# Postnorm decoder layer on one core: the norms' products moved to VectorE, later weights' roundings to ScalarE, and the side stages placed anew

## The chip, the cores and the metric

One core of a Trainium2 chip runs the whole layer in one launch. The metric is the device time of that launch in microseconds (us), lower is better. The engines are PE (TensorE, matrix products and transposes), DVE (VectorE), ACT (ScalarE), POOL (GpSimd) and SP (SyncE, which only issues DMAs). Each engine works through its own instruction queue in the order in which the program was written; they meet only at semaphores.

## What is computed

For x of shape (4, 512, 512), with a layer norm (mean and variance over the last axis, no weights) behind each of three parts:

```python
x = layernorm(x + attention(x, Wq, Wk, Wv, Wo))          # 32 heads of 64, 8 kv heads, rope, causal softmax
x = layernorm(x + experts(x, fside, ctx))                # one int8 "smooth quant" expert per batch
x = layernorm(x + ffn(x, sign(up), sign(down), scales))  # 512 -> 2048 -> 512, relu
```
```python
def smooth_quant_linear(x, w):
    s = sqrt(max(amax|x| over rows, EPS) / max(amax|w| over rows, EPS)), at least EPS
    xs, ws = x / s, w * s
    x_scale, w_scale = max(amax of each row of |xs|, |ws|, EPS) / 127
    x_q, w_q = clip(round(xs / x_scale)), clip(round(ws / w_scale))
    return x_q @ w_q.T * x_scale * w_scale.T
# expert: h = smooth_quant_linear(x, fside); a = silu(gate) * up; smooth_quant_linear(a, ctx)
```

## The kernel before

Products that need more than one pass are made of a high part and a low part (`_hi`, `_lo`): ACT copies the high part, DVE or POOL subtracts it from the full value to get the low part, and PE multiplies the pairs.

**Attention** goes through 16 steps `g`: eight key/value heads for batches 0 and 1 (`half` 0), then the same eight for batches 2 and 3 (`half` 1). A step has two batches `b` and four query heads `h`, so 128 heads in all. In each head PE transposes the last head's probabilities (`ps_t`, L1752), makes the next head's scores (`ps_s`, L1707), a piece of the output projection into the bank `m1`, a projection into `m0`, and the products with the values (`ps_o`, L1764). DVE, in each head: `pT_lo` (L1433) three times, the row maxima of the next head's scores (`probs,neg_max`, L1372, `softmax_max`) four times, two of them before and two of them behind the second and third `pT_lo`; `add_o` (L1380); `add_y`, which adds a piece of the output projection to `y` (L1395); the inverse sums `r_inv` (L1455); and, by head, `normalize` (L1386) and the rotations of q. ACT takes the exponentials (L1162) and the high parts. POOL does the low parts of q, k, the weights and the output (`o_lo`, L980), the rotations of k, and `r_rep` (L964). Once a half of a pair of heads is done, PE spreads its inverse sums into the bank `m1` (`recips`, L1774); that product waits until `add_y` has read the bank.

**The side chains.** While half 1 of the attention runs, the 64 heads of it are "ticks" 0 to 63, and the layer norm and the expert of batches 0 and 1 are worked in between. The chain `N` of a batch is its first norm: `var0` to `var3` and `rstd` on DVE, `power` (the inverse root, L1091) on POOL, and `norm0` to `norm3`, the product `(y - mean) * rstd` of 128x512 each (`centered`, L1037) on POOL. `A` is the first linear of the expert: `wmax` of the transposed weights, `colmax` of `y`, `colx`, `ratio`, `root`, `reps`, `rowsw`, `rowsx`, the scaled `xs` (DVE) and `ws` (POOL), their row maxima `xabs`, `wabs`, the scales, the roundings `xround` and `wround` (add and scale, L1034 on POOL, L1255 on ACT), `xq`, `wq` (DVE), transposes `xT`, `wT` on PE, and four `prod`. `B` is the second linear with the same stages in half the width, then `add` (POOL), `var2`, `rstd2` (DVE), `power` and `y20` to `y23` (POOL, the second norm's product by the same `centered`), and `x2T0` to `x2T3` on PE with `hi` on ACT and `lo` (L1639) on DVE, which make the transposed input of the feed forward.

Tables of text give the tick and the place of each stage; `PLACED` puts them together, and each engine's function `later(place, tick)` emits what the table has there. For DVE the place `dve` lies in the middle of a head, between the first `pT_lo` and the second, and `dve2` behind the inverse sums:

```python
if k == 0 and half == 1:
    later("dve", slot(g, b, h))
```

**The feed forward** follows. For each of four batches it has 16 hidden tiles, so that two ticks (64 on) are one tile: eight `up` matmuls of 128x512 into `m0` (L1994), `hid` and `hid_hi` on ACT, `hid_lo` on POOL (L1030), and eight `down` matmuls into `ps_s` and `ps_t` (L2008) one tick later. `T` is the rest of the output projection of batch 3, `S` the signs of the weights, and `F` the last norm of a batch (`scale` DVE, `add` POOL L1105, `var` DVE, `power` POOL, `norm` DVE L1678, store). The chains of batches 2 and 3 (`A2`, `B1`, `A3`, `B2`, `B3`) run beside the tiles; the up matmuls of batch b wait for the last `lo` of `B` of that batch. `feed` emits the tiles, then `later` the stages of the tick.

Small operations on 128x4 or 128x2 (`scales` L1483, `ratio`, `reps` L1495, `inverse`, `variance`) are `tensor_scalar` with a constant, followed by a reciprocal or a product.

## Time and profile before

| | |
|---|---|
| median of 3 runs | 1498.04 us (1497.72 to 1505.10) |
| profiled execution | 1497.09 us |
| its span, first to last instruction | 1495.3 us |
| mean granted PE clock over the span | 0.964 of full speed |
| busy in the span | PE 1315.8 (88%), weight loads 1085.3, DVE 972.3 (65%), ACT 891.4 (60%), POOL 860.7 (58%) |
| heads 0 to 63 (half 0) | 0 to 560.5 us |
| heads 64 to 127 (half 1, ticks 0 to 63) | 560.5 to 1128.6 us |
| feed forward | 1128.6 to 1495.3 us |

A time beside a name is the start of an instruction from the span's start. An instruction's idle time is that of its engine just before it, with the one whose semaphore came last. Matmuls overlap: one of 128x512 is shown with 0.39 us, and the next starts 0.23 us after it. The profile's granted clock is 1.0 at 2.4 GHz and 0.5 at 1.2 GHz.

### The profile page before, as it was taken

How to read it: one execution, taken by the hardware profiler on the slowest of the kernel's cores; microseconds unless marked ns; L12 is line 12 of the kernel's file. 1: busy time of each engine (PE TensorE's matmuls, PEld its weight loads, DVE VectorE, ACT ScalarE, POOL GpSimd, SP SyncE). 2: the span in 40 equal slices, each digit the busy share in tenths (PEclk: the TensorE clock that was granted, in tenths of full speed). 3: DMA queues.
4: the chain of work that ended last, by engine and by line, in shares of the span. 5: the costliest groups of instructions: out<-in, count | busy, mean ns of one | idle time of the engine just before them, and what ended most of it. 6: DMA issues, size and time to landing. Idle time of an engine off the chain costs nothing.

```text
span 1495.3 us, 25046 instructions
## 1 busy us (share of the span) xinstructions
PE 1315.8 (88%) x7112; PEld 1085.3 (73%) x7112; DVE 972.3 (65%) x2391; ACT 891.4 (60%) x2120; POOL 860.7 (58%) x735
## 2 busy tenths in 40 slices
PE   3799999999999999899998999988879577988896
PEld 2688878888788877777787877776767455676675
DVE  3477777677777668788877878768765627634022
ACT  2576777767776766666776666655665453433332
POOL 3465565565664765756784555585514764747443
PEclk9899999999999999999999999999989798999998
DMA  4422222222222223212222223212234011100000
GB/s 177 149 77 50 59 57 72 75 54 56 56 67 63 77 86 106 57 50 61 54 76 63 68 80 88 61 48 52 54 137 184 1 43 43 43 14 29 0 29 28
DMA packets 54853, 98.78 MB, mean 66 GB/s; under 512 B 11744, under 2 KB 13792, under 8 KB 53728
## 3 DMA queue, kind: packets, MB, share of 16 engines
q1 hardware_dynamic: 54752, 97.57, 22.8%
q8 instruction: 47, 0.77, 0.2%
q14 instruction: 54, 0.44, 0.1%
HBM read 51.39 MB, written 4.19 MB: 37 GB/s over the span
## 4 chain that ended last, share of the span: by engine, by line
PE 56%; DVE 13%; POOL 13%; issue 9%; ACT 7%; DMA 0%; DVEq 0%; ACTq 0%; POOLq 0%; SPq 0%
PE m L1707 21%; PE ps_o L1764 7%; PE ps_s L1707 7%; PE m L1994 5%; PE ps_t L1752 5%; POOL y L1037 3%; PE ps_s L2008 3%; DVE probs L1372 3%; PE ps_t L2008 3%; DVE pT_lo L1433 2%; ACT pT_hi L1170 2%; PE m L1774 2%; POOL y L1105 1%; POOL o_lo L980 1%; ACT probs L1162 1%
## 5 line engine op out<-in xcount | busy, mean ns | idle before, releaser
L1162 ACT ACTIVATE probs<-probs,neg_max 128x128 f32<-128x128 f32 (+3 forms) x512 | 285.2, 559 | 192.6 <-DVE neg_max L1372 192.4
L1433 DVE TENSOR_TENSOR pT_lo<-ps_t,pT_hi 128x512 fp32r<-128x512 f32 (+1 forms) x384 | 220.1, 595 | 180.4 <-ACT pT_hi L1170 178.3
L1372 DVE CUSTOM_DVE_ANT_0 probs<-ps_s,mask 128x128 f32<-128x128 f32 (+3 forms) x512 | 228.3, 482 | 6.5 <-PE ps_s L1707 6.2
L1752 PE MATMUL ps_t<-ident,probs 128*128 128x128 f32 x1280 | 187.6, 278 | 50.3 <-DVE pT_lo L1433 29.3
L1707 PE MATMUL ps_s<-k_st,q_st 128*128 128x256 f32 (+2 forms) x1024 | 231.0, 348 | 0.3 <-DVE neg_max L1372 0.3
L980 POOL TENSOR_TENSOR o_lo<-o_sum,o_hi 128x512 fp32r<-128x512 f32 x64 | 81.9, 1280 | 223.0 <-ACT o_hi L1184 222.8
L1752 PEld LDWEIGHTS ps_t<-ident,probs 128*128 128x128 f32 x1280 | 148.4, 142 | 75.7 <-DVE pT_lo L1433 39.3
L1170 ACT ACTIVATE pT_hi<-ps_t 128x512 fp32r<-128x512 f32 (+1 forms) x384 | 186.1, 519 | 8.6 <-PE ps_t L1752 5.3
L1764 PE MATMUL ps_o<-pT_hi,v_st 128*128 128x256 f32 (+2 forms) x512 | 171.9, 346 | 2.1 <-DVE pT_lo L1433 2.1
L1030 POOL TENSOR_TENSOR hid_lo<-hid,hid_hi 128x512 fp32r<-128x512 f32 x64 | 82.2, 1287 | 136.6 <-ACT hid_hi L1337 136.6
L1764 PE MATMUL ps_o<-pT_lo,v_st 128*128 128x256 f32 (+2 forms) x512 | 157.6, 329 | 0.0
L1707 PEld LDWEIGHTS ps_s<-k_st,q_st 128*128 128x128 f32 x1024 | 151.6, 191 | 3.0 <-DVE neg_max L1372 0.5
L1335 ACT ACTIVATE hid<-m,up_col 128x512 f32<-128x512 f32 x64 | 43.9, 686 | 149.7 <-PE m L1994 149.7
L1177 ACT ACTIVATE o_part<-ps_o 64x512 f32<-64x512 f32 x128 | 75.8, 592 | 78.5 <-PE ps_o L1764 76.1
L1707 PE MATMUL m<-xT_hi,wqT_hi 128*128 128x512 f32 x256 | 102.2, 399 | 16.7 <-DVE xT_lo L1400 15.1
L1707 PE MATMUL m<-woT_hi,o_hi 128*128 128x512 f32 x256 | 106.0, 414 | 10.0 <-POOL o_lo L980 5.4
L1764 PEld LDWEIGHTS ps_o<-pT_hi,v_st 128*128 128x128 f32 x512 | 99.0, 193 | 13.0 <-DVE pT_lo L1433 3.4
L1764 PEld LDWEIGHTS ps_o<-pT_lo,v_st 128*128 128x128 f32 x512 | 99.2, 194 | 7.5
L1707 PE MATMUL m<-xT_hi,wqT_lo 128*128 128x512 f32 x256 | 101.9, 398 | 0.0
L1707 PE MATMUL m<-xT_lo,wqT_hi 128*128 128x512 f32 x256 | 101.8, 398 | 0.0
L1707 PE MATMUL m<-woT_lo,o_hi 128*128 128x512 f32 x256 | 101.6, 397 | 0.0
L1707 PE MATMUL m<-woT_hi,o_lo 128*128 128x512 f32 x256 | 101.5, 397 | 0.0
(246 smaller groups left out, 3111.3 us busy)
## 6 DMA issues: line engine op xcount, KB each, us to landing
q_st<-q_tmp SPq DMA_DIRECT2D x512, 64.0 KB, 2.0
raw<-in_wq_t SPq DMA_DIRECT2D x32, 256.0 KB, 3.0
k_st<-k_st SPq DMA_DIRECT2D x64, 128.0 KB, 2.3
raw<-in_wo_t SPq DMA_DIRECT2D x32, 256.0 KB, 2.9
raw_b<-in_ffn_t SPq DMA_DIRECT2D x10, 512.0 KB, 7.1
y<-in_x_t SPq DMA_DIRECT2D x4, 1024.0 KB, 9.5
raw<-in_wkv_t SPq DMA_DIRECT2D x16, 256.0 KB, 3.5
y<-in_x SPq DMA_DIRECT2D x4, 1024.0 KB, 6.1
```

The costliest lines, as they stand in the source:

```text
L980: pool.tensor_tensor(o_lo[:, buf, p, :], o_sum[:, :], f32(o_hi[:, buf, p, :]), ALU.subtract).then_inc(o_los, 1)
L1030: pool.tensor_tensor(hid_lo[:, n % 2, :], hid[:, n % 2, :], f32(hid_hi[:, n % 2, :]), ALU.subtract).then_inc(hid_los, 1)
L1162: act.activation(probs[:, h % 2, SO[i]:SO[i] + SW[i]], probs[:, h % 2, SO[i]:SO[i] + SW[i]], ACT.Exp, bias=neg_max[:, h % 2, i:i + 1], sca ...
L1170: act.activation(pT_hi[:, PT_FIRST[k]:PT_FIRST[k] + w, :], ps_t[:, (h + k) % 2, 0:P * w].rearrange("p (w c) -> p w c", c=P), ACT.Copy).the ...
L1177: act.activation(o_part[a:a + HD, :], ps_o[c:c + HD, :], ACT.Copy).then_inc(o_copied, 1)
L1372: dve.tensor_tensor_reduce(out=probs[:, h % 2, SO[i]:SO[i] + SW[i]], in0=ps_s[:, i % 2, 0:SW[i]], in1=mask[:, L - SW[i]:L], scale=-SCALE, ...
L1433: dve.tensor_tensor(pT_lo[:, d, :], ps_t[:, (h + k) % 2, 0:P * w].rearrange("p (w c) -> p w c", c=P), f32(pT_hi[:, d, :]), ALU.subtract).t ...
L1707: i = pe.matmul(dst, a, c, start=(j == 0), stop=(j == len(terms) - 1))
L1752: i = pe.transpose(ps_t[:, (h + k) % 2, P * c:P * (c + 1)], probs[:, h % 2, at:at + P], ident[:, :])
L1764: i = pe.matmul(ps_o[:, q0:L], v_st[:, buf, kt, v0:v0 + P], pT[:, blocks, :], start=(j == 0 and s == 0), stop=(j == 3 and s == 1))
L1994: i = pe.matmul(m0[:, :], w[:, P * k:P * (k + 1)], x2[:, b % 2, k, :], start=(k == 0 and x2 is xT_hi), stop=(k == KT - 1 and x2 is xT_lo))
L2008: i = pe.matmul(down_bank(t), hd[:, m % 2, P * t:P * (t + 1)], w[:, D:2 * D], start=(h == 0 and hd is hid_hi), stop=(h == HT - 1 and hd is ...
```

## The change

1. `centered` is emitted on DVE, not on POOL: the products `norm0` to `norm3` of all four `N` chains and `y20` to `y23` of all four `B` chains, 32 of 128x512. POOL keeps `power`. `x2T` of a tile waits for that tile's `y2` alone, where it waited for `y23`.
2. `wround` of batches 2 and 3 of `A` (8 of 128x512) and of batches 1 to 3 of `B` (12 of 128x256) goes from POOL to ACT.
3. The place `dve` in the middle of a head is gone. `dve1` is behind the inverse sums, `dve2` at the end of the head. On PE `pe1` is new, at a head's start; `pe2` and `pe3` are the old `pe` and `pe2`. POOL's places are as they were, but for that of the third head, which follows that of the second.
4. Small operations with a constant read it from a tile `bounds` and are `tensor_tensor`; `scales` has one more of them.
5. Stages are cut finer: `xs`, `xabs` and `wabs` of `A` by 512 columns, `xq`, `wq` and `a` in two, all of `B`'s `colmax`, `xs`, `xabs`, `wabs` in two, and `scale`, `add`, `var`, `norm` of `F` in four.
6. `inv_a` has two buffers, so that `wmax` of `A1` runs before `A0`'s weights are reloaded (`A1.wT` at tick 7, `A0.w` at 11). Waits for the shared bank `pc` are worked out from the table (`PC_USES`, `pc_free`).
7. The two tables `ATTENTION` and `FEED_FORWARD` take the place of all the old ones; nearly every stage has another tick.

```diff
-            def centered(n, mv, inv, t):
-                return pool.tensor_scalar(y[:, n, :], y[:, n, :], mv[:, t, 0:1], inv[:, 1, t:t + 1], ALU.subtract, ALU.mult)
...
+            def centered(n, mv, inv, t):
+                return dve.tensor_scalar(y[:, n, :], y[:, n, :], mv[:, t, 0:1], inv[:, 1, t:t + 1], ALU.subtract, ALU.mult)
...
                             if k == 0 and (prev or h > 0):
                                 add_o(n - 1, (h - 1) % G, u * 2 + (h - 1) // 2)
-                            if k == 0 and half == 1:
-                                later("dve", slot(g, b, h))
...
                         dve.reciprocal(r_inv[:, :, h // 2, h % 2], row_sum[:, h % 2, :]).then_inc(r_done, 1)
                         if half == 1:
-                            later("dve2", slot(g, b, h))
+                            later("dve1", slot(g, b, h))
...
                             if b == 0 and prev:
                                 add_y(g, b, half, "out3 early")
+                        if half == 1:
+                            later("dve2", slot(g, b, h))
...
+                elif name[:6] == "wround":
+                    after(act, "A", "dve", b, "wscale")
+                    i = scale_round(w_gu, sm_a, 7, [int(name[6])], D)
...
             def scales(sm, j):
-                link(dve.tensor_scalar(sm[:, j, :], sm[:, j, :], EPS, 1.0 / QMAX, ALU.max, ALU.mult))
+                link(dve.tensor_tensor(sm[:, j, :], sm[:, j, :], bound(0, QT), ALU.max))
+                link(dve.tensor_tensor(sm[:, j, :], sm[:, j, :], bound(1, QT), ALU.mult))
                 return dve.reciprocal(sm[:, j + 1, :], sm[:, j, :])
...
             def reps(sm, kt):
-                link(dve.tensor_scalar(sm[:, 3, 0:kt], sm[:, 3, 0:kt], EPS, None, ALU.max))
+                link(dve.tensor_tensor(sm[:, 3, 0:kt], sm[:, 3, 0:kt], bound(0, kt), ALU.max))
...
                     t = int(name[3])
-                    if t == 0:
-                        after(pe, "B", "pool", b, "y23")
+                    after(pe, "B", "dve", b, f"y2{t}")
...
-    47 pool power y20
-    48 pool y21 y22
-    50 pool y23
+    50 dve1 B0.y20
+    50 dve2 B0.y21
+    50 pool1 B0.power
+    51 dve1 B0.y22
+    51 dve2 B0.y23
```

Three places of the order show it. DVE, attention, the head in which the stage `reps` of `A1` stands before (tick 48): `L1380` is `add_o`, `L1495` and `L1496` are the stage, `L1433` the second and third `pT_lo`, `L1372` the last maxima, `L1395` `add_y`, `L1455` the inverse sums. Before:

```order
L1380 TENSOR_TENSOR o_sum<-ps_o,o_part 64x512
L1495 TENSOR_SCALAR sm_a<-sm_a 128x4
L1496 RECIPROCAL sm_a<-sm_a 128x4
L1433 TENSOR_TENSOR pT_lo<-ps_t,pT_hi 128x512
L1433 TENSOR_TENSOR pT_lo<-ps_t,pT_hi 128x256
L1372 ISA probs,neg_max<-ps_s,mask 128x384
L1372 ISA neg_max 128x1
L1372 ISA probs,neg_max<-ps_s,mask 128x512
L1372 ISA neg_max 128x1
L1395 TENSOR_TENSOR y<-y,m 128x512
L1455 RECIPROCAL r_inv<-row_sum 128x4
L1386 TENSOR_TENSOR o_sum<-o_sum,m 128x512
```

The same head in the change (its lines are `L1538`, `L1476`, `L1499`, `L1558`, `L1490`; the stages there now are `xs` of `A1`, `L1658`):

```order
L1538 TENSOR_TENSOR pT_lo<-ps_t,pT_hi 128x256
L1476 ISA probs,neg_max<-ps_s,mask 128x384
L1476 ISA neg_max 128x1
L1476 ISA probs,neg_max<-ps_s,mask 128x512
L1476 ISA neg_max 128x1
L1499 TENSOR_TENSOR y<-y,m 128x512
L1558 RECIPROCAL r_inv<-row_sum 128x4
L1658 TENSOR_TENSOR xs<-y,pc 128x512
L1490 TENSOR_TENSOR o_sum<-o_sum,m 128x512
L1459 TENSOR_TENSOR q_tmp<-m,sin_sb 128x512
L1460 TENSOR_TENSOR q_tmp<-m,cos_sb 128x512
L1658 TENSOR_TENSOR xs<-y,pc 128x512
```

The stage stood ahead of the maxima and of `add_y`; now one stands behind the inverse sums and one behind all of the head's own work.

POOL, feed forward, first batch: `L1049` scales the weights of `A2`, `L1074` and `L1075` those of `B1`, `L1091` and `L1037` are `power` and the products of `N3`, `L1030` is `hid_lo`, `L1034` `wround`. Before:

```order
L1049 TENSOR_TENSOR w_gu<-w_gu,cm 128x512
L1074 TENSOR_TENSOR w_dn<-w_dn,cm_b 128x256
L1075 TENSOR_TENSOR w_dn<-w_dn,cm_b 128x256
L1091 TENSOR_TENSOR norm_n<-norm_n,half_pow 128x4
L1037 TENSOR_SCALAR y<-y,mv_n,norm_n 128x512 x4
L1049 TENSOR_TENSOR w_gu<-w_gu,cm 128x512
L1030 TENSOR_TENSOR hid_lo<-hid,hid_hi 128x512
L1034 TENSOR_SCALAR w_gu<-w_gu,sm_a 128x512 x2
L1034 TENSOR_SCALAR w_dn<-w_dn,sm_b 128x256 x4
```

In the change (`L1152`, `L1177` and `L1178`, `L1136` in the same roles):

```order
L1164 TENSOR_TENSOR sm_b<-sm_b,half_pow 128x2
L1152 TENSOR_TENSOR w_gu<-w_gu,cm 128x512 x2
L1136 TENSOR_TENSOR hid_lo<-hid,hid_hi 128x512
L1177 TENSOR_TENSOR w_dn<-w_dn,cm_b 128x256
L1178 TENSOR_TENSOR w_dn<-w_dn,cm_b 128x256
L1177 TENSOR_TENSOR w_dn<-w_dn,cm_b 128x256
L1178 TENSOR_TENSOR w_dn<-w_dn,cm_b 128x256
L1136 TENSOR_TENSOR hid_lo<-hid,hid_hi 128x512
L1152 TENSOR_TENSOR w_gu<-w_gu,cm 128x512
```

The products of the norm and the roundings are no longer between the scalings and `hid_lo`.

PE, feed forward, end of the first batch, in the change: `L2043` are products of `A2`, `L1984` all four `x2T` of `B1`, `L2105` the first up matmuls of the next batch. Before, each `x2T` (`L1861`, four transposes) had eight matmuls of a tile between it and the next.

```order
L2043 MATMUL m<-wqT,xqT 128x512 x4
L2043 MATMUL ps_o<-wqT,xqT 128x512 x4
L1984 MATMUL pc<-ident,y 128x128 x16
L2105 MATMUL m<-xT_hi,sgn_a 128x512
L2105 MATMUL m<-xT_lo,sgn_a 128x512
```

The four now stand behind each other, with no tile between.

## Rows read from the trace of the kernel before

**Rows 1.** Windows (steady step, half 1): length, PE, PEld, DVE, ACT, POOL busy (instructions), clock, DMA
```profile
240.60:304.00 63.40, 61.10 (x355) 52.24 (x353) 45.97 (x127) 45.10 (x117) 36.55 (x31) 1.00 0.24 62
560.50:1128.60 568.10, 509.93 (x2903) 427.05 (x2901) 433.28 (x1105) 373.63 (x945) 335.47 (x285) 0.97 0.26 72
```
**Rows 2.** Waits of the steady step: us in total, times, longest
```profile
DVE pT_lo L1433 <- ACT pT_hi L1170: 10.3, 9, 2.1
ACT probs L1162 <- DVE neg_max L1372: 9.5, 11, 1.3
```
**Rows 3.** Waits of half 1 of the attention
```profile
ACT probs L1162 <- DVE neg_max L1372: 116.5, 98, 7.5
DVE pT_lo L1433 <- ACT pT_hi L1170: 92.6, 62, 4.1
PE m L1774 <- DVE y L1395: 23.8, 16, 5.7
```
**Rows 4.** Timeline, head at tick 48: start, us, engine, line, [idle before]
```profile
982.96 4.12 POOL L1037 TENSOR_SCALAR y<-y,mv,norm 128x512 f32<-128x512 f32 x2
988.12 1.23 DVE L1495 TENSOR_SCALAR sm_a<-sm_a 128x4 f32<-128x4 f32 x1 [4.73 <-POOL sm_a L1042]
991.12 0.61 ACT L1162 ACTIVATE probs<-probs,neg_max 128x384 f32<-128x384 f32 x1 [7.51 <-DVE neg_max L1372]
992.35 1.12 PE L1774 MATMUL m<-ident,r_rep 128*128 128x128 f32 x4 [5.65 <-DVE y L1395]
```
**Rows 5.** Timeline, head at tick 53: a small stage of A1 and POOL's work beside it
```profile
1033.62 4.01 DVE L1483 TENSOR_SCALAR sm_a<-sm_a 128x4 f32<-128x4 f32 x1
1035.09 2.51 POOL L952 TENSOR_TENSOR q_tmp<-q_tmp 128x512 fp32r<-128x512 f32 x2
```
**Rows 6.** Windows of the feed forward: the four batches of tiles
```profile
1128.60:1253.00 124.40, 92.14 (x426) 69.03 (x427) 65.32 (x105) 55.02 (x76) 70.26 (x55) 0.86 0.18 68
1253.00:1340.30 87.30, 78.00 (x374) 58.54 (x372) 49.70 (x78) 36.82 (x56) 56.64 (x49) 0.95 0.07 25
1340.30:1421.10 80.80, 70.00 (x306) 54.01 (x305) 25.59 (x44) 28.16 (x45) 45.83 (x38) 0.94 0.04 14
1421.10:1478.50 57.40, 55.75 (x241) 44.94 (x240) 10.16 (x17) 19.77 (x31) 25.19 (x20) 1.00 0.05 19
```
**Rows 7.** Timeline of the feed forward: POOL, DVE and PE
```profile
1179.27 8.25 POOL L1037 TENSOR_SCALAR y<-y,mv_n,norm_n 128x512 f32<-128x512 f32 x4
1188.77 1.22 DVE L1487 TENSOR_REDUCE sm_a<-w_gu 128x2 f32<-128x1024 f32 x1 [9.23 <-POOL w_gu L1049]
1191.58 1.03 PE L1868 MATMUL ps_o<-ident,xq 128*128 128x128 bf16 x8 [13.85 <-DVE xq L1557]
1232.48 1.11 PE L1861 MATMUL pc<-ident,y 128*128 128x128 f32 x4 [8.73 <-POOL y L1037]
1235.95 0.63 PE L2008 MATMUL ps_t<-sgn_b,hid_hi 128*128 128x512 f32 x1
1249.17 0.80 PE L1994 MATMUL m<-xT_hi,sgn_a 128*128 128x512 f32 x1 [5.16 <-DVE xT_lo L1639]
1313.14 0.80 PE L2008 MATMUL ps_s<-sgn_b,hid_hi 128*128 128x512 f32 x1 [3.48 <-POOL hid_lo L1030]
```
**Rows 8.** Waits of the feed forward
```profile
PE ps_s L2008 <- POOL hid_lo L1030: 15.9, 6, 6.1
PE pc L1868 <- DVE xq_b L1614: 3.8, 2, 3.5
```
**Rows 9.** Instructions by line: ns min/median/max, first and last start
```profile
L1037 POOL TENSOR_SCALAR y<-y,mv_n,norm_n x16: 2066/2074/3130, 613.6 to 1185.4; 128x512 f32<-128x512 f32 x16
L1678 DVE TENSOR_SCALAR y<-y,mv_f,norm_f x16: 533/546/1585, 1283.4 to 1491.6; 128x512 f32<-128x512 f32 x16
L1255 ACT ACTIVATE xs<-xs,round_col,sm_a x8: 798/802/816, 1173.2 to 1272.8; 128x512 f32<-128x512 f32 x8
L1492 DVE TENSOR_TENSOR sm_a<-sm_a,inv_a x4: 161/162/166, 652.5 to 1255.8; 128x4 f32<-128x4 f32 x4
L1573 DVE TENSOR_TENSOR av_f<-xs x3: 1207/1216/1706, 1160.0 to 1307.9; 128x1024 f32<-128x1024 f32 x3
```

1061 lines of the change are left out of this document (582 added, 479 removed).

## The prediction

> **What bounds the kernel now.** I read the windows first, then the waits, then the timeline around the longest of them. PE is the engine that sets the end wherever the others keep up. A steady step of half 0 takes 63.40 us and PE is busy for 61.10 of them [rows 1], so there is nothing to win in half 0, which the change hardly touches. Half 1 takes 568.10 us where eight steady steps would take 8 x 63.4 = 507.2: an excess of 60.9. PE's own busy time is 509.93 against 8 x 61.10 = 488.8, so 21.1 of the excess is work of the side chains (and some slow clock), and 39.8 is PE standing still more than it does in half 0.
>
> The feed forward takes 1495.3 - 1128.6 = 366.7 us. PE is idle for 124.4 - 92.1 = 32.3, then 9.3, 10.8 and 1.7 us in the four batches of tiles [rows 6]: 54 us. Its mean granted clock there is 0.86, 0.95, 0.94 and 1.00, so some of the busy time is at the lower level of 1.2 GHz. The last 16.8 us, behind 1478.5, are the last norm and its store. Together PE waits for about 94 us that other engines could in principle cover, and the question is how much of it this change removes.
>
> *Attention.* The waits of half 1 [rows 3] hold one that belongs to the place of the stages: the spread of the inverse sums waits for `add_y` 16 times, 23.8 us in all. The head at tick 48 shows how [rows 4]. POOL works on `y2` products, so `root` is late; the stage `reps`, in the middle of DVE's head, waits 4.73 us for it and takes 1.23; the third and fourth maxima and `add_y` stand behind it; ACT waits 7.51 for a maximum and PE 5.65 for `add_y`. ACT's wait for maxima is 116.5 us in half 1, against 9.5 x 8 = 76 at the steady rate [rows 2, 3]: 40 more, which agrees with PE's 39.8.
>
> *Feed forward.* The two largest stops are in the first batch [rows 7]. POOL does the four products of `N3` in 8.25 us between two scalings of `A2`'s weights; DVE waits 9.23 for the scaling, and PE 13.85 for an `xq` that stands behind it. 41 us later PE waits 8.73 for the four `y2` of `B1`. After each, PE's matmuls run at 1.2 GHz for a while: the one at 1235.95 takes 0.63 us instead of 0.39.
>
> **The change, part by part.** The sum is made against the profiled execution, 1497.09 us; the median of the three runs is 0.95 above it.
>
> *The place in the head.* With `dve1` behind the inverse sums and `dve2` behind the whole head, no stage of a head stands before that head's maxima or `add_y`. I take the whole 23.8 us of PE's wait for `add_y` as gone. What the moved stages now delay is `normalize`, the rotation of q, and the next head's first `pT_lo`. DVE is idle before `pT_lo` for 10.3 us in a steady step, 1.3 a head [rows 2], and for 92.6 in half 1, because the late exponentials only move that idle time [rows 3]. That is the cover. The table puts up to three `xs` at one head's end, and some ten heads are over 1.3 us by about 0.4, so I give back 4 us. Without the cover all the stages' time would come back: DVE is busy for 433.28 us in half 1, 8 x 45.97 = 367.8 of it the attention's own, so 65.5 us of stages [rows 1].
>
> *The products on DVE.* In attention 12 of them leave POOL at 2.07 us each, 24.8 us. On DVE the same operation is there already in the last norm: median 0.55, at worst 1.59 [rows 9]. 12 cost 6.6 to 19 us of DVE, beside the same idle time. I take the lower end for the clock and nothing for the path, since they stand at heads' ends; the upper end goes into the range. `reps` no longer waits behind `y2` at tick 48, which is a part of the 23.8 and is not counted again. Attention: 23.8 - 4 = 20 us less.
>
> *First batch of tiles.* POOL loses the 8.25 us of `N3` between the scalings, and `A2`'s transposes stand nine ticks later, so the 13.85 goes. The 8.73 becomes the first `y2` alone, 0.55 to 1.59 us. After both stops eight matmuls ran 0.43 us apart instead of 0.23, 1.6 us each time. That is 13.85 + 8.73 - 1 + 3.2 = 24.8. Against it stand the four `x2T` in one place: each needs PE, then ACT, then DVE before the bank is free, and DVE has other stages between the four `lo`. By the order PE would be idle there for about 7 us and slow after it, where it was idle 1.3 + 5.16 before [rows 7]. With 2 us more there and some of the gain lost to stages that are late for another reason, I take 20.
>
> *Other batches.* PE waits 15.9 us for `hid_lo` in six places [rows 8]. The two longest, 6.1 and the one at 1313.14 with 3.48 [rows 7], are behind `y2` products, and go: 9.6. The rest is mostly behind the four `add` of the last norm, which now stand apart: half of it, 2.6. `xq_b` is 3.8, nearly all in one wait behind `ws`, and clock after the 6.1 another 1.8. That makes 17.8; I take 16. The end of 16.8 us stays. Feed forward: 36 us less.
>
> *The roundings on ACT.* 8 of 128x512 at 0.80 us [rows 9], and 12 of half the width that cost no more: below 16 us on an engine that is busy for 120 of 292 us in the first three batches of tiles [rows 6]. `hid` needs about 1.3 us per tile, and the roundings are one to four in a tick. Nothing on the path, if `wscale` is done when ACT comes to them; if it isn't, `hid` waits, the more so because the whole tile waits for it.
>
> *Small operations.* The one at 1033.62 took 4.01 us while POOL ran operation after operation [rows 5]; an undisturbed `tensor_tensor` of that size takes 0.16 [rows 9]. On the path I count nothing beyond the 23.8 in which it is. **The Trainium skill**, page "SBUF — State Buffer", section "Who interferes with whom", says that DVE shares a port pair with GpSimd, that a two-port mode takes it, and that an instruction with two SBUF inputs contends as well with a GpSimd instruction that reads SBUF, the loser being fully blocked. By that rule the new small `tensor_tensor`, with two SBUF inputs, would wait as the old ones did, and the product at 0.55 us would wait whenever POOL works. Rows 9 hold both: no slower small `tensor_tensor` than 0.166 us, but one of 128x1024 at 1.71 instead of 1.21.
>
> Sum: 1497.09 - 20 - 36 = 1441; with the median's 0.95 I predict **1442 us**.
>
> **Rivals.**
> - *Only POOL's stops go.* The stages at heads' ends cost as much as those in the middle: each is still DVE time between one head's exponentials and the next head's `pT_lo`. For it: DVE's 433 of 568 us leave little, and the table puts more stages into the first 32 heads than before. Against it: in the old place even a short stage holds ACT and PE [rows 4]. Attention then gains 5, the feed forward 20, since the four `x2T` in one place and `hid` behind the roundings take the rest: 1497 - 25 = 1472.
> - *PE comes near its floor.* Stages placed apart on all engines leave no long stop: 36 of the 39.8 in attention and 50 of the 54 in the feed forward go, 1497 - 86 = 1411. For it: hardly any stop is a true dependence, most are queue order. Against it: the chain from `A1` to `x2T` of `B1` must still fit into one batch of tiles.
> - *The products starve on DVE, slower.* 32 products that POOL never had to wait with are now of the kind that took up to 1.59 us beside POOL [rows 9], and a small one took 4.01 beside back-to-back POOL work [rows 5]. If a product takes 2.9 us instead of 0.55 and stands on the path, 32 x 2.35 = 75 us come back, and 1441 becomes 1516. It decides from 0.55 + 56/32 = 2.3 us per product on. Against it: POOL has 66 us less to do, and 15.9 of the waits of PE were behind POOL. The skill's rule of full blocking speaks for this case, and its time is the one given here.
> - *The stages in effect stay where they were* (a place moved, waits turned into others of equal length): 1490 to 1505, slightly either way.
>
> **How the numbers follow.** The forecast, 1425 to 1460, has 0.60. PE near its floor has 0.14, only POOL's stops 0.14, no net change 0.05, starved products 0.07. The predicted time is that of the first. The range must leave out no more than 2 in 10: from 1415, which cuts off about half of the floor's case, to 1480, which takes in the second end of POOL's case and leaves out the last two. A measurement of this kernel can tell about 0.5%, 7.5 us, from no change. Faster by more than that: 0.60 + 0.14 + 0.14 and a little of the rest, 0.89; within it 0.04; slower 0.07.
>
> **What would show it.** In the changed kernel's profile the spread of the inverse sums (the product from `r_rep`) should wait for `add_y` for under 5 us in all, half 1 should take about 548 us and the first batch of tiles about 104, with the others at 80, 72 and 57. No POOL group for the products, 48 products by the line of `centered` on DVE with a mean below 1.2 us. The four `x2T` of `B1` should show PE idle for 6 to 8 us. Small operations should be at 0.2 us with no 4 us among them. I am wrong if half 1 takes over 560 us, or if the mean product is above 2.3 us, or if ACT's `hid` shows waits behind its own roundings with PE idle for it.

## The result, and the profile after

The changed kernel takes **1410.45 us** (median of 4 runs, 1408.63 to 1410.71), beside 1501.57 us (1497.72 to 1506.46) for the kernel before on the same chip: a ratio of 0.9389, 95% interval 0.9353 to 0.9425. The forecast was 1442 with a range of 1415 to 1480, so the sign was right, the size was not, and the time lies below the range. It is the time that the rival "PE comes near its floor" gave (1411, chance 0.14). The profiled execution took 1410.46 us, span 1408.6, mean granted clock 0.981 for 0.964 before. Stretches and waits below are each of one execution, and executions of one kernel differ by up to 12 us (1463.93 to 1475.62 in e5; the profiled one of before, 1497.09, is at the low end of its own), so by stretches the gain is 86.7 us and by the ratio 92.

The windows of the changed kernel: half 1, the four batches of tiles and the end, in the columns of [rows 1, 6].

```profile
563.60:1100.70 537.10, 500.23 (x2890) 423.17 (x2894) 447.93 (x1141) 374.83 (x945) 310.42 (x273) 0.98 0.28 74
1100.70:1197.40 96.70, 87.97 (x430) 66.01 (x434) 79.20 (x138) 59.84 (x84) 40.76 (x35) 0.96 0.28 99
1197.40:1270.90 73.50, 72.95 (x371) 57.37 (x373) 55.99 (x99) 41.46 (x63) 43.66 (x37) 0.99 0.09 29
1270.90:1336.30 65.40, 64.97 (x305) 51.50 (x305) 31.28 (x54) 29.93 (x48) 35.98 (x30) 1.00 0.05 17
1336.30:1391.80 55.50, 55.50 (x242) 45.09 (x241) 10.01 (x17) 19.81 (x30) 25.45 (x20) 1.00 0.05 19
1391.80:1408.60 16.80, 3.92 (x16) 2.56 (x15) 7.86 (x17) 1.32 (x2) 7.23 (x6) 0.76 0.17 62
```

Half 1 is 31.0 us shorter (568.1 to 537.1), the feed forward 58.8 (366.7 to 307.9): batch by batch 27.7, 13.8, 15.4 and 1.9, the end of 16.8 unchanged. Half 0 is 3.1 longer (560.5 to 563.6), but that isn't the change's: kernels below with the same half 0 took 561.8 to 564.7. Two things fell at once. PE's idle time went from 58.2 to 36.9 us in half 1 and from 54.0 to 9.7 in the four batches. And its busy time fell, for the same matmuls: 509.93 to 500.23 in half 1, and by 14.5 in the batches.

The waits of half 1, then those of PE in the feed forward (total, times, longest), which answer to [rows 3, 8]:

```profile
ACT probs L1257 <- DVE neg_max L1476: 75.2, 85, 3.4
DVE pT_lo L1538 <- ACT pT_hi L1265: 55.9, 53, 3.0
PE ps_t L1873 <- DVE pT_lo L1538: 20.3, 18, 3.7
PE m L1895 <- DVE y L1499: 4.2, 2, 2.4
...
PE pc L1984 <- DVE xT_lo L1759: 4.9, 3, 1.9
PE m L2105 <- DVE xT_lo L1759: 1.8, 2, 1.4
PE ps_s L2119 <- POOL hid_lo L1136: 1.0, 1, 1.0
```

The wait of the spread of the inverse sums for `add_y` has gone from 23.8 to 4.2 us, and ACT's for the maxima is down to the steady rate of 76. PE's 15.9 us behind `hid_lo` are down to 1.0, and the 13.85 behind `xq` and the 8.73 behind `y2` are gone. What is left in the feed forward is the turn of the four `x2T`. What is new is PE's wait for `pT_lo`, 20.3 us with stops up to 3.7; before it was 14.9. Three heads, at ticks 5, 21 and 37, take 12.35, 12.0 and 12.5 us where a head of their kind takes 6.65.

### The profile page after: what moved, and what is told of

Read it like the earlier page. It is cut to its first block, busy times and chain, and to the rows that moved or that the text cites. A ratio compares the mean times of both kernels' runs of the same rounds, so it can differ in the third digit from the quotient of the medians.

```text
span 1408.6 us, 25177 instructions
## 1 busy us (share of the span) xinstructions
PE 1293.1 (92%) x7101; PEld 1075.5 (76%) x7112; DVE 1012.7 (72%) x2491; ACT 904.2 (64%) x2140; POOL 783.6 (56%) x686
## 4 chain that ended last, share of the span: by engine, by line
PE 75%; DVE 9%; ACT 6%; issue 5%; POOL 3%; DMA 1%; ACTq 0%; DVEq 0%; SPq 0%; POOLq 0%
PE m L1828 30%; PE ps_s L1828 9%; PE ps_o L1885 8%; PE m L2105 7%; PE ps_t L1873 7%; PE ps_s L2119 4%; PE ps_t L2119 3%; DVE pT_lo L1538 2%; PE m L1895 2%; ACT pT_hi L1265 2%; ACT probs L1257 1%; DVE o_sum L1490 1%; PE pc L1984 1%; DVE probs L1476 1%; POOL o_lo L1087 1%
## 5 line engine op out<-in xcount | busy, mean ns | idle before, releaser
L1538 DVE TENSOR_TENSOR pT_lo<-ps_t,pT_hi 128x512 fp32r<-128x512 f32 (+1 forms) x384 | 220.7, 595 | 143.4 <-ACT pT_hi L1265 141.2
L1476 DVE CUSTOM_DVE_ANT_0 probs<-ps_s,mask 128x128 f32<-128x128 f32 (+3 forms) x512 | 228.2, 482 | 6.6 <-PE ps_s L1828 6.6
L1885 PE MATMUL ps_o<-pT_hi,v_st 128*128 128x256 f32 (+2 forms) x512 | 168.7, 340 | 0.2 <-DVE o_sum L1484 0.2
L1136 POOL TENSOR_TENSOR hid_lo<-hid,hid_hi 128x512 fp32r<-128x512 f32 x64 | 83.0, 1297 | 133.7 <-ACT hid_hi L1441 133.6
L1828 PE MATMUL m<-xT_hi,wqT_hi 128*128 128x512 f32 x256 | 102.6, 401 | 18.3 <-DVE xT_lo L1504 16.7
## 6 DMA issues: line engine op xcount, KB each, us to landing
raw_b<-in_ffn_t SPq DMA_DIRECT2D x10, 512.0 KB, 6.8
```

Of the source, the lines that this page charges most:

```text
L1136: pool.tensor_tensor(hid_lo[:, n % 2, :], hid[:, n % 2, :], f32(hid_hi[:, n % 2, :]), ALU.subtract).then_inc(hid_los, 1)
L1476: dve.tensor_tensor_reduce(out=probs[:, h % 2, SO[i]:SO[i] + SW[i]], in0=ps_s[:, i % 2, 0:SW[i]], in1=mask[:, L - SW[i]:L], scale=-SCALE, ...
L1538: dve.tensor_tensor(pT_lo[:, d, :], ps_t[:, (h + k) % 2, 0:P * w].rearrange("p (w c) -> p w c", c=P), f32(pT_hi[:, d, :]), ALU.subtract).t ...
L1828: i = pe.matmul(dst, a, c, start=(j == 0), stop=(j == len(terms) - 1))
L1885: i = pe.matmul(ps_o[:, q0:L], v_st[:, buf, kt, v0:v0 + P], pT[:, blocks, :], start=(j == 0 and s == 0), stop=(j == 3 and s == 1))
```

## The experiments

Ratios are to the kernel before, run beside it. The stretches are of the profiled execution, in us; a batch is one of tiles. By "the table" is meant what the change did to the order of the stages beside the parts with a name: their ticks, the finer cuts and the waits worked out from them.

| kernel | ratio (95%) | half 0 | half 1 | batch 0 | batch 1 | batch 2 |
|---|---|---|---|---|---|---|
| before | 1 | 560.5 | 568.1 | 124.4 | 87.3 | 80.8 |
| changed | 0.9389 (0.9353 to 0.9425) | 563.6 | 537.1 | 96.7 | 73.5 | 65.4 |
| e1, norms on POOL | 0.9508 (0.9480 to 0.9536) | 562.6 | 542.2 | 103.8 | 77.8 | 72.2 |
| e2, roundings on POOL | 0.9420 (0.9395 to 0.9444) | 563.1 | 537.0 | 98.3 | 76.4 | 65.3 |
| e3, place in mid head | 0.9606 (0.9580 to 0.9631) | 564.7 | 571.3 | 96.8 | 73.4 | 65.4 |
| e4, unstarved | 0.9305 (0.9281 to 0.9329) | 564.1 | 527.0 | 96.9 | 73.2 | 65.4 |
| e5, before + place | 0.9784 (0.9739 to 0.9829) | 562.0 | 536.6 | 124.0 | 92.5 | 82.6 |
| e6, before + products | 0.9772 (0.9743 to 0.9801) | 563.5 | 561.3 | 110.7 | 87.1 | 72.1 |
| e7, before + three parts | 0.9646 (0.9616 to 0.9675) | 561.8 | 539.7 | 112.2 | 85.9 | 72.1 |
| e8, e1 and e2 together | 0.9554 (0.9520 to 0.9587) | 564.0 | 537.0 | 106.9 | 79.8 | 72.3 |
| e9, e4 + x2T between | 0.9298 (0.9279 to 0.9317) | 563.8 | 527.1 | 95.2 | 74.6 | 65.4 |
| e10, e4 + x2T later | 0.9278 (0.9256 to 0.9299) | 564.7 | 525.5 | 96.6 | 72.7 | 65.4 |
| e11, reduction at the place | 0.9344 (0.9321 to 0.9367) | 563.4 | 533.4 | 97.0 | 73.4 | 65.4 |
| e12, small constants | 0.9378 (0.9359 to 0.9397) | 563.7 | 539.8 | 96.1 | 72.2 | 65.4 |
| e13, eight stops in half 0 | 0.9551 (0.9527 to 0.9574) | 587.5 | 538.1 | 96.8 | 73.5 | 65.4 |
| e14, e7 + A2's xT later | 0.9635 (0.9609 to 0.9661) | 563.5 | 538.4 | 114.7 | 85.7 | 72.0 |
| e15, combined | 0.9298 (0.9275 to 0.9321) | 564.3 | 523.6 | 95.3 | 74.9 | 65.4 |
| e16, e14 + B1's xT later | 0.9662 (0.9631 to 0.9694) | 562.3 | 538.4 | 117.4 | 82.9 | 72.1 |
| e17, combined, one more | 0.9274 (0.9250 to 0.9299) | 563.3 | 523.4 | 95.5 | 74.1 | 65.4 |

### The place in the head

e3 puts VectorE's first place back, e5 gives it to the kernel before.

```diff
                             if k == 0 and (prev or h > 0):
                                 add_o(n - 1, (h - 1) % G, u * 2 + (h - 1) // 2)
+                            if k == 0 and half == 1 and slot(g, b, h) > 0:
+                                later("dve1", slot(g, b, h))
...
-                        if half == 1:
+                        if half == 1 and slot(g, b, h) == 0:
                             later("dve1", slot(g, b, h))
```

> The changed kernel with VectorE's first place of a head moved back to where it was before the change, behind the first lo part of the probabilities and ahead of the inverse sums (all heads but the first of the second half). Theory: the wait of the recips' transposes for add_y and of the probabilities for the maxima of the next head come back, as in the sum of the prediction: +15 to +25 us, all of it between 564 and 1101 us, none in the feed-forward. Rival B (the table, not the place): within 5 us of 1410. Rival D (the place costs in both directions, what is late is then the stages themselves): over +30.

> The kernel before with one part of the change alone: VectorE's first place of a head behind the inverse sums and the second at the head's end; tables, products, roundings and small operations stay as before. In the changed kernel the place was worth 34 us (the first place moved back gave half 1 of 571 us for 537). Theory (the place alone ends the waits behind add_y and the maxima, whatever the table): half 1 of 568 us goes to 540 to 548, so 20 to 28 us less than before, ratio 0.981 to 0.987. Rival G (place and table only work together, since stages that PE awaits in the same head are now late): within 5 us of before, or slower.

e3 lost 34.2 us in half 1 and e5 won 31.5, each with nothing else in half 1 changed, so **the place is worth all of the attention's 31.0 us**, and more than the prediction's theory or either expectation gave it. By its size e3 lands at its rival D, over 30 us, but 11.8 of the 34.2 are PE's busy time (512.0 for 500.2); its idle time rose by 22.4, which is within the 15 to 25 of the theory. PE's waits in e3's half 1, and the windows of half 1 in e5:

```profile
PE ps_t L1875 <- DVE pT_lo L1538: 21.5, 16, 4.3
PE m L1897 <- DVE y L1499: 18.3, 15, 3.5
```

```profile
562.00:1098.70 536.70, 500.25 (x2904) 422.42 (x2903) 426.32 (x1105) 374.46 (x945) 334.89 (x285) 0.98 0.27 75
```

The wait for `add_y` is there again with 18.3 us. In e5 PE's idle time falls from 58.2 to 36.5, by 21.7, close to what the prediction took (23.8 less 4); its busy time falls by 9.7 as well. But e5 lost 5.2 us in batch 1 and 1.8 in batch 2 without any change there. For batch 1 the traces show what goes with it, one small operation, the scale of `A3`; batch 2's stays open. Before, then e5, with POOL's last two operations beside it:

```profile
1268.48 0.72 DVE L1483 TENSOR_SCALAR sm_a<-sm_a 128x4 f32<-128x4 f32 x1
1238.13 3.88 DVE L1483 TENSOR_SCALAR sm_a<-sm_a 128x4 f32<-128x4 f32 x1
1239.45 2.52 POOL L1049 TENSOR_TENSOR w_gu<-w_gu,cm 128x512 f32<-128x512 f32 x2
```

It ends 0.03 us after POOL does. PE's two stops at the transposes of `xq_b` and `xq` behind it grow from 3.54 and 0.44 us to 4.08 and 2.10, and PE's busy time in the batch by 2.9. So that loss goes with an operation held beside POOL, as in the three long heads below. e7 and e14 have the same 3.88 us in a batch 1 of 85.9 and 85.7 us; e16 hasn't, in one of 82.9.

### The products, the roundings, the small operations

e1 moves the 32 products of the first norms and of the norms behind B back to POOL's queue, e2 the roundings of A2, A3 and B1 to B3, e8 both; e12 takes back the form of the small operations. Some lines of each table, and one of the operations:

```diff
 e1
-    94 pool1 B1.power
-    95 dve1 A3.wmax1 A2.prod1 B1.y20 B1.y21 B1.y22
+    94 pool1 B1.power B1.y20 B1.y21 B1.y22 B1.y23
+    95 dve1 A3.wmax1 A2.prod1
 e2
-    88 act1 B1.wrow A2.xround3 A2.wround0 A2.wround1
-    88 pool1 B1.add0
+    88 act1 B1.wrow A2.xround3
+    88 pool1 A2.wround0 A2.wround1 B1.add0
 e12
-                link(dve.tensor_tensor(sm[:, j, :], sm[:, j, :], bound(0, QT), ALU.max))
-                link(dve.tensor_tensor(sm[:, j, :], sm[:, j, :], bound(1, QT), ALU.mult))
+                link(dve.tensor_scalar(sm[:, j, :], sm[:, j, :], EPS, 1.0 / QMAX, ALU.max, ALU.mult))
```

> The changed kernel with one part undone: the 16 products of the first norms and the 16 of the norms behind the attention layers' second product go back to POOL, at the tick of their power; all other stages stay where the change put them. Theory (each of three parts removes stops of its own: products off POOL, the place in the head, the finer table): in the feed-forward half 24 products of 1.25 us stand before hid_lo again, so PE stops there; +10 to +20 us over the changed kernel's 1410, while two of the three long heads (12.3 us instead of 6.65) lose their cause, -11, and bursts of five POOL operations delay o_lo by some us each in two places. Sum: about 1420, between 1412 and 1430. Rival A (most of the gain is the products leaving POOL): 1455 or more. Rival B (the table alone gives the gain): 1400 to 1412.

> The changed kernel with the later layers' weight roundings (A2, A3, B1, B2, B3: 8 of 512 columns and 12 of 256) back on POOL at the same ticks, ahead of the additions there; nothing else. Theory: POOL gets about 8 x 1.25 + 12 x 0.65 = 18 us back in bursts of 1.3 to 2.5 us, each ahead of one hid_lo; about half shows as PE's wait: +8 us, 1418, with no change before 1100 us. Rival C (the roundings on ScalarE are a main part of the feed-forward's 59 us): +25 us or more. Rival B (the table alone): within 3 us of 1410.

> The changed kernel with the norms' products and the later layers' weight roundings both back on POOL. Alone they cost 19 and 3 to 5 us. Theory: they stand in the same queue ahead of hid_lo, in bursts of different ticks, so the sum: 22 to 26 us over the changed kernel, 1435 to 1440 (ratio to before 0.955). Rival J (POOL is near its limit in the feed-forward, so the second costs more than alone): 32 us or more.

> The changed kernel with the small operations as before: bounds and scales by constants in tensor_scalar (two bounds in one operation in the scales) instead of tensor_tensor with a tile of bounds. Theory (the form is worth nothing, as in the prediction's sum, since either form waits beside POOL): within 3 us of 1410 (ratio 0.937 to 0.941), with the long head at tick 37 as before. Rival M (the form by constants takes longer beside POOL, as the one of 4.01 us did): 6 us or more slower, small operations over 1.3 us in over six places.

e1 costs 18.1 us in the feed forward, as expected (there by 20 products of 2.07 us, not by the 24 of 1.25 of the expectation), and its half 1 took 5.1 more, where 11 less were expected: two of the long heads did go, but POOL's burst made another, of 17.6 us. The 5.1 themselves are not the products': e8 has the same program in half 1 and took 537.0 there. PE's waits in e1's feed forward, then POOL and VectorE in its head 3:

```profile
PE ps_s L2116 <- POOL hid_lo L1122: 12.5, 4, 4.7
PE pc L1981 <- DVE xT_lo L1756: 4.5, 3, 1.5
```

```profile
585.56 8.26 POOL L1129 TENSOR_SCALAR y<-y,mv_n,norm_n 128x512 f32<-128x512 f32 x4
593.78 1.26 POOL L1073 TENSOR_TENSOR o_lo<-o_sum,o_hi 128x512 fp32r<-128x512 f32 x1
595.15 0.68 DVE L1481 TENSOR_TENSOR o_sum<-ps_o,o_part 64x512 f32<-64x512 f32 x1 [6.54 <-POOL o_lo L1073]
```

Four products in one tick take 8.26 us, and whatever the path needs of POOL stands behind them: `hid_lo` there, as before the change [rows 8], and `o_lo` here, for which VectorE waits 6.54 us. e2 costs 4.5 us of feed forward. e8 costs 23.4 there, where the two alone make 22.6 (by the ratios 25 us in all, where they make 22.5), so they add up and rival J's 32 did not come. The small operations' form changes nothing that can be measured (e12): the one at the end of head 36 takes 3.27 us as a `tensor_scalar` and 3.26 as a `tensor_tensor`.

### The parts one by one from the other side

e6 gives the kernel before the products alone, e7 the products, the roundings and the place, with before's ticks and unsplit stages.

```diff
 N_FAST
-    2 pool power norm0 norm1 norm2 norm3
+    2 pool power
+    3 dve norm0 norm1 norm2 norm3
 B_FAST
-    8 pool wround0 wround1
+    8 act wround0 wround1
-    18 pool power y20 y21 y22 y23
+    18 pool power
+    19 dve y20 y21 y22 y23
```

> The kernel before with the norms' 32 products of y on VectorE, in the tick behind their power or the next ones, and nothing else. In the changed kernel they are worth 18 us of the feed-forward and 5 of the attention. Theory: the same here, feed-forward 366.7 to about 348, attention between -5 and +5 (products at VectorE's middle place delay the maxima by 0.55 us each): 18 to 25 us less than before, ratio 0.984 to 0.988. Rival A (with before's coarser table POOL's bursts of five cost more): 30 us or more. Rival H (products in the middle of a head starve as at ticks 4 and 20 of the changed kernel): attention 5 us or more longer for each.

> The kernel before with three parts of the change together: place, products on VectorE, later layers' roundings on ScalarE; before's table of ticks, stages unsplit, small operations by constants. What is left to the changed kernel is the table alone (finer stages, other ticks, waits for a bank's readers) and the small operations. Theory: place -25, products -20, roundings -4, sum 50 of the 92 us; the table is worth the other 40, nearly all in the feed-forward (ratio 0.966). Rival B' (the table gives under 10 us, and the three parts do together what they don't do alone): ratio 0.945 or less. Rival I (the table is nearly all): ratio 0.985 or more.

The products give 22.6 us of the feed forward (366.7 to 344.1) and 6.8 of half 1. Together that is 29 us, by the ratio of 0.9772 even 34, more than the 18 to 25 expected and about rival A's 30: with before's places the products cost more than in the changed kernel. Roundings add nothing in e7 (344.4 for 344.1), as far as two kernels can tell that each hold one small VectorE operation in batch 1, for 6.60 us in e6 and 3.88 in e7. With place, products and roundings the kernel has 53 of the 92 us; what is left is **the table: 36.5 us of the feed forward** (344.4 to 307.9), and 2.6 net in half 1, where it also made the three long heads. This was expected at 40, and e12 shows that the small operations have no share in it.

Which property of the table it is, e14 and e16 asked. In e7 PE stands 8.2 us at A2's `xT`, which it meets before VectorE has its `xq`. e14 places that stage five ticks later (with it `xq` three, `wq` and `wT` two and what follows one tick), e16 also B1's `xT` three ticks later (`wT` and `wrow` one).

```diff
-    10 pe xT0 xT1
-    11 act wround2 wround3 xqT0 xqT1
+    11 act wround2 wround3
+    15 pe xT0 xT1
+    15 act xqT0 xqT1
 B_FAST, for B1, in e16
-    8 pe xT
+    11 pe xT
```

> The kernel before with the three parts (ratio 0.9646, first batch of tiles 112.2 us), and in its table one chain delayed: A2's xT from tick 81 to 86, xq from 80 to 83, wT, wrow and the products behind it by one tick; nothing else. Theory (the table's gain is that PE meets no stage before its data are there; in before's table it meets A2's xT 8.2 us early): the 8.2 us stop is gone or under 2 us, half of it comes back as a denser end of the batch, first batch 104 to 108 us, ratio 0.959 to 0.962. Rival O (the chain itself is too long, and the wait moves to a later stage of it): within 2 us of 112.

> The kernel before with the three parts, A2's transposes later as in the run before (ratio 0.9635), and now B1's as well: its xT from tick 81 to 84, wT from 84 to 85, wrow from 85 to 86, products as before. Theory (PE meets both chains' stages before VectorE has got to them, so only both together help): 3 more ticks are about 7 us of tiles, the 9.15 us stop falls to 2 or less, first batch 114.7 to 106 to 109 us, ratio 0.957 to 0.960. Rival P (VectorE's queue from tick 72 to 92 is the bound of the batch, whatever PE's order; the wait moves to the products or x2T): first batch 112 to 116 us.

Both failed. In e14 the stop became one of 9.15 us at B1's `xT`; in e16 that one is gone too, and batch 0 is 117.4 us, longer than before either move. ScalarE's timeline in e16 shows what holds it now:

```profile
1150.36 2.08 ACT L1325 ACTIVATE av_f<-av_f,round_col,sm_b 128x256 f32<-128x256 f32 x4 [2.36 <-DVE sm_b L1561]
1152.34 1.04 ACT L1394 ACTIVATE sgn_b<-raw_b 128x1024 fp32r<-128x1024 f32 x1
1153.28 0.67 ACT L1412 ACTIVATE hid<-m,up_col 128x512 f32<-128x512 f32 x1
```

ScalarE meets the roundings before VectorE's scales are there, and `hid` stands behind them; it is the same again 6 us later, and PE waits 4.51 and 2.34 us for the two `hid`. That is what the prediction feared of the roundings; the changed kernel has no such wait of PE. So PE's early stage was one symptom of before's ticks, and two attempts to move single stages sent the stop to another engine's queue. That all the ticks are too early on every engine is a reading of these two runs and not shown. Whether the split of the stages or their ticks carries more of the 36.5 us stays open; it was not tried apart.

### The three long heads

The changed kernel at head 4's end: VectorE, POOL and PE from its timeline.

```profile
604.78 3.52 DVE L1618 TENSOR_SCALAR y<-y,mv_n,norm_n 128x512 f32<-128x512 f32 x1
608.23 0.68 DVE L1538 TENSOR_TENSOR pT_lo<-ps_t,pT_hi 128x512 fp32r<-128x512 f32 x1
...
604.31 1.27 POOL L1087 TENSOR_TENSOR o_lo<-o_sum,o_hi 128x512 fp32r<-128x512 f32 x1
605.55 1.25 POOL L1053 TENSOR_TENSOR q_tmp<-q_tmp 128x512 f32<-128x512 f32 x1
606.77 1.25 POOL L1054 TENSOR_TENSOR q_tmp<-q_tmp 128x512 f32<-128x512 f32 x1
...
608.96 0.69 PE L1873 MATMUL ps_t<-ident,probs 128*128 128x128 f32 x2 [3.59 <-DVE pT_lo L1538]
612.28 0.63 PE L1828 MATMUL m<-woT_lo,o_hi 128*128 128x512 f32 x1
```

The product starts 0.47 us after POOL's `o_lo` and ends 0.28 after the last of three POOL operations that follow each other without a gap. PE stands for 3.59 us, and then its matmul of 512 columns takes 0.63 instead of 0.39. At 741.15 the same happens again, and at 881.06 it happens to the scale of the down layer, a `tensor_tensor` of 128x4 (minimum, median, maximum of its line in ns):

```profile
L1618 DVE TENSOR_SCALAR y<-y,mv_n,norm_n x16: 516/541/3523, 592.8 to 1138.9; 128x512 f32<-128x512 f32 x16
L1591 DVE TENSOR_TENSOR sm_b<-sm_b,bounds x8: 151/340/3264, 881.1 to 1291.9; 128x4 f32<-128x4 f32 x8
```

e4 moves the three stages off that place, which lies behind the rotation of the queries; e11 leaves two and puts a reduction where the first stood.

```diff
 e4
-    4 dve2 N0.norm3
-    5 dve1 A0.wmax1
+    5 dve1 N0.norm3 A0.wmax1
-    20 dve2 N1.norm1
-    21 dve1 N1.norm2
+    21 dve1 N1.norm1 N1.norm2
-    36 dve2 B0.xscale
-    37 dve1 B0.wabs0
+    37 dve1 B0.xscale B0.wabs0
 e11
-    4 dve2 N0.norm3
-    5 dve1 A0.wmax1
+    4 dve2 A0.wmax1
+    5 dve1 N0.norm3
```

> The changed kernel with three stages moved by one place, from the end of a head to behind the inverse sums of the next: the fourth norm product of batch 0, the second of batch 1, and the scale of the down layer. Each of them began in the changed kernel while POOL ran two or three operations in a row behind the rotation of the queries and ended only after the last (3.52, 3.52 and 3.26 us instead of 0.54 and 0.16), and the head behind it took 12.0 to 12.5 us instead of 6.65. Theory (VectorE is starved there by POOL, and all of the long head comes from it): three heads of 6.65, -15 to -17 us, about 1394. Rival E (the op is long because what it reads or the queue is late, so the delay moves along): -5 us or less. Rival F (the ops are starved at the new place as well): no change.

> The changed kernel with two stages exchanged: at the end of head 4, behind the rotation of the queries, stands the maximum of weights A0.wmax1 (a reduction with one input from SBUF, 128x512 twice, about 1.2 us), and the fourth norm product stands where the maximum was, behind the inverse sums of head 5. Theory (what starves there is an operation with two inputs from SBUF or in the fast form, not any operation): the reduction runs its 1.2 us while POOL works, head 5 takes 6.7 to 7.6 us instead of 12.35, and the kernel 5 us less. Rival F' (whatever stands there is late while POOL runs three operations in a row): the reduction takes over 3 us and the head 12 or more.

e11, VectorE and POOL at the same place:

```profile
604.55 1.22 DVE L1626 TENSOR_REDUCE inv_a<-w_gu 128x2 f32<-128x1024 f32 x1
605.80 0.69 DVE L1538 TENSOR_TENSOR pT_lo<-ps_t,pT_hi 128x512 fp32r<-128x512 f32 x1
...
604.10 1.27 POOL L1087 TENSOR_TENSOR o_lo<-o_sum,o_hi 128x512 fp32r<-128x512 f32 x1
605.33 1.26 POOL L1053 TENSOR_TENSOR q_tmp<-q_tmp 128x512 f32<-128x512 f32 x1
```

The reduction starts in the middle of the same POOL work and isn't held: 1.22 us, and head 5 takes 7.31 us. Nor is, in the changed kernel, an `xs` with one input from PSUM at head 48's end:

```profile
984.42 0.69 DVE L1658 TENSOR_TENSOR xs<-y,pc 128x512 f32<-128x512 f32 x1
...
983.81 1.29 POOL L1087 TENSOR_TENSOR o_lo<-o_sum,o_hi 128x512 fp32r<-128x512 f32 x1 [0.24 <-ACT o_hi L1279]
985.05 1.31 POOL L1053 TENSOR_TENSOR q_tmp<-q_tmp 128x512 f32<-128x512 f32 x1
```

So it is the kind of operation that decides, at a place where POOL is busy. **The Trainium skill**, page "SBUF — State Buffer", section "Who interferes with whom", says that a `tensor_reduce` never contends on trn2, that an operation with two SBUF inputs and a `tensor_scalar` in a two-port mode can, and that the loser is fully blocked. Both timelines agree with it; which mode the products ran in no trace shows. Two inputs aren't needed: the same scale as a `tensor_scalar` with constants took 3.27 us (e12).

Nor is it the end of a head: the 4.01 us of [rows 5] stood in the middle of one, and e5's 3.88 and e6's 6.60 among the tiles. Over all the runs 25 such operations (small ones and products) took more than 3 us. Beside each of them POOL ran from one operation into the next, three to seven of them, and each ended 0.02 to 0.29 us after POOL's last. Nothing here shows why VectorE gets in between two POOL operations at other times.

In e4 all three heads are at 6.65 us or so, 17 us less, but half 1 fell by only 10.1: head 38, behind the scale that was moved, takes 10.39 us instead of 8.77, and the last 16 heads took 129.9 us where the changed kernel took 125.4. PE's stops there are of the same size in both (about 2.1, 1.8, 1.9 and 2.4 us). Windows of the same heads, 58 and 59, in the changed kernel and then in e4:

```profile
1054.50:1074.20 19.70, 13.93 (x93) 11.92 (x93) 13.88 (x36) 13.42 (x33) 4.02 (x4) 1.00 0.66 189
```

```profile
1040.40:1063.20 22.80, 17.05 (x92) 14.73 (x93) 13.99 (x36) 13.50 (x33) 3.96 (x4) 0.85 0.61 183
```

Idle time is the same, 5.8 us, and busy time 3.1 more at a clock of 0.85. It need not be another kernel for that. e1 and e8 have the same program in half 1; their windows of it:

```profile
562.60:1104.80 542.20, 502.07 (x2894) 424.59 (x2892) 434.85 (x1129) 375.09 (x945) 334.33 (x285) 0.98 0.28 74
564.00:1101.00 537.00, 496.84 (x2895) 419.66 (x2894) 434.95 (x1129) 375.19 (x946) 334.43 (x285) 0.99 0.28 74
```

PE is idle for 40.1 and 40.2 us, and busy for 5.2 more in e1, whose five executions lie at 1427 to 1428 us and at 1432 to 1433. The same stops cost the clock in one execution and not in another. So the 4.5 us of e4 can't be put down to what was moved, though its five executions agree within 1.8 us.

### What a stop costs

That led to e13: eight equal delays in half 0, where nothing else is in the way.

```diff
+                        if half == 0 and (b, h) == (1, 1):
+                            for j in range(6):
+                                dve.tensor_reduce(sm_b[:, j, 0:1], sin_sb[:, :], AX.X, ALU.max)
```

> The changed kernel with a known delay in half 0 alone: at the end of VectorE's seventh-last place, head 1 of the second fill in each of its eight steps, six added reductions of 128x512 from one SBUF tile (0.65 us each, 3.9 us, written to a tile that is overwritten later). VectorE is idle there for about 1.3 us, so PE should stand still for about 2.6 us eight times, 21 us. Theory (a stop costs more than itself, since the matmuls behind it run at 1.2 GHz for a while): half 0 takes 3.6 to 4.3 us more for each, 29 to 34 us in all, and PE's busy time in it rises by 5 to 12 us although its work is the same. Rival N (a stop costs its length or less): 21 us or less, PE's busy time the same within 2 us.

The six reductions took 3.64 us, and the stop was 1.91 us at seven of the eight places and 2.66 at the last; 2.6 was expected. Half 0 took 23.9 us more. The windows of e13 behind two of the stops, at 105.4 and at 171.4, and PE's timeline behind the second:

```profile
105.40:109.40 4.00, 4.00 (x18) 3.06 (x18) 3.94 (x13) 2.47 (x8) 0.00 (x0) 1.00 0.43 98
171.40:175.40 4.00, 3.99 (x14) 3.23 (x15) 3.94 (x13) 2.46 (x8) 0.00 (x0) 0.68 0.46 107
```

```profile
171.41 0.44 PE L1876 MATMUL ps_t<-ident,probs 128*128 128x128 f32 x2 [1.91 <-DVE pT_lo L1538]
172.54 0.40 PE L1831 MATMUL m<-xT_hi,wkvT_hi 128*128 128x512 f32 x1
173.59 0.63 PE L1831 MATMUL m<-xT_hi,wkvT_hi 128*128 128x512 f32 x1
```

Behind the first stop the clock stays at 1.00 and the head takes 10.60 us instead of 8.32: 2.3 more. Behind the second it falls to 0.68 over 4 us, a part of them at 1.2 GHz, and the head takes 11.98: 3.7 more. They alternate: four heads of the eight lost 2.3, three 3.7, the last 2.7. The windows from the head of the first stop to the end of half 0, in the changed kernel and in e13:

```profile
99.70:563.40 463.70, 445.80 (x2558) 380.00 (x2557) 333.52 (x914) 330.01 (x854) 273.38 (x233) 1.00 0.26 66
100.60:587.30 486.70, 452.70 (x2558) 382.39 (x2557) 361.29 (x962) 329.95 (x854) 273.63 (x233) 0.99 0.25 63
```

PE's idle time rose by 16.1 us (17.9 to 34.0) and its busy time by 6.9, for the same matmuls. **A stop of PE costs itself and, on average, two fifths more.** The theory had that right, in kind and in size: it asked for 5 to 12 us of busy time. The 29 to 34 us of half 0 did not come since the stops were shorter.

### Versions that beat both

e9 fills the turn of B1's four `x2T` with two products, e10 moves batch 0's `x2T` to PE's second place, e15 has both and the scale beside its `xabs1`, and e17 one stage more.

```diff
 e9
-    95 pe1 A2.prod2 A2.prod3 B1.x2T0 B1.x2T1 B1.x2T2 B1.x2T3
+    95 pe1 B1.x2T0 A2.prod2 B1.x2T1 A2.prod3 B1.x2T2 B1.x2T3
 e10
-    58 pe1 B0.x2T0
-    58 pe2 A1.wT0
-    58 act1 B0.hi0
-    58 dve1 B0.lo0
+    58 pe2 A1.wT0 B0.x2T0
+    58 act2 B0.hi0
+    58 dve2 B0.lo0
 e15
-    36 dve1 B0.xabs1
+    36 dve1 B0.xabs1 B0.xscale
 e17
-    97 pe1 B2.colx A3.colx
+    97 pe1 B2.colx
+    98 pe1 A3.colx
```

> The kernel with the three stages moved (1399 us here, ratio 0.9305), and in it the turn of batch 1's second norm: PE's last two products of A2 between the first three transposes x2T instead of ahead of all four, VectorE's four norm products ahead of them and its other stages behind the last lo, ScalarE's silu behind the four hi. Theory (each x2T stops PE for 1.4 to 1.85 us since it waits for ScalarE's hi and VectorE's lo of the one before, 6.3 us in all, and two stops can be filled with a product of 0.9 us each): 1.8 to 3.5 us less in batch 1's first tile (18.2 us) and up to 1 at 1.2 GHz, about 1396. Rival K (the chain is bound by VectorE's four norm products, which then stand ahead of it): no change or up to 2 us more.

> The kernel with the three stages moved (ratio 0.9305), and in it the four transposes x2T of batch 0 at PE's second place of heads 58 to 61 instead of the first, with their hi at ScalarE's and their lo at VectorE's end of the head. Theory (the first x2T waits 2.1 us at the head's start for the bank that v's lo part frees late, the fourth 1.1 for the lo before): 3 us less in heads 58 to 61 of 36.4 us. Rival L (the heads 58 to 62 lack work on PE, since the last step projects nothing for a next one, so a stop that is taken away comes back at the spread of the inverse sums, which waits 1.8 and 2.4 us for the sum of y): within 1 us of 1399.

> The changed kernel with all stages moved that the runs named: the three starved ones (the down layer's scale now beside its xabs1 in head 36, since at head 37 it made head 38 1.6 us longer), the four x2T of batch 0 at PE's second place, and the turn of batch 1's norm with two products between its x2T, B2's column maxima ahead of A3's. Theory: 1397.5 - 1.6 for head 38, - 1.7 for the first batch and no loss in the second: about 1394, between 1391 and 1397. Rival (ScalarE, the clock or other waits take it back, as heads 58 to 62 took 4.5 of 17 us): 1397 to 1400.

> The combined kernel (1397.6 us, ratio 0.9298) with the spread of A3's column maxima one tick later on PE, tick 98 instead of 97: it stood still there for 2.07 us. Theory: 1.5 to 2.1 us less in the second batch (74.9), about 1395.7, ratio 0.9285. Rival: within 0.5 us of the combined kernel, since the stop goes to the next stage.

e9 won 1.7 us in batch 0 and lost 1.4 in batch 1, so nothing. e10 won 1.5 us of half 1 where 3 were expected: two stops went, and the spread of the inverse sums waits 2.50 instead of 1.80, as its rival said. e15 came out at 1397.55, at the rival's time: half 1 was the best yet (523.6), but a new stop of 2.07 us stood in batch 1. e17 takes it away and has 1394.93 us (1394.68 to 1395.72), 0.9274 of before and 0.988 of the changed kernel by the two ratios. Its batch 1 is only 0.8 us shorter than e15's. Against e10, with a ratio of 0.9278, the lead is within the intervals. Its window of half 1:

```profile
563.30:1086.70 523.40, 495.73 (x2896) 419.07 (x2894) 439.62 (x1141) 374.36 (x945) 310.76 (x273) 0.99 0.28 76
```

## Why the prediction was wrong in size

*What bounds the kernel.* Right: half 0 had nothing to give, the stops of PE were where the gain lay, and the rows that were named as the largest (the wait for `add_y`, 13.85, 8.73, `hid_lo`) are those that went.

*Where it failed, first: the clock.* The step that failed is the term for PE's busy time. The sum took stops at their own length and added 3.2 us for the first batch ("eight matmuls ran 0.43 us apart instead of 0.23, 1.6 us each time") and 1.8 for the others; for the attention it added nothing. PE's busy time fell by 9.7 us in half 1 and 14.5 in the four batches, 24.2 against 5: **19 us of the error.** The mean granted clock in the batches rose from 0.86, 0.95 and 0.94 to 0.96, 0.99 and 1.00. Across kernels with the same matmuls in half 1, idle and busy time go together: 59.3 and 512.0 in e3, 58.2 and 509.9 before, 36.9 and 500.2 changed, 29.9 and 497.1 in e4, 27.7 and 495.7 in e17. 31.6 us less idle time went with 16.3 less busy time. e13 shows it caused, at two fifths; e1 and e8 show that 5 us of busy time come and go at the same idle time, so the share for one kernel is no closer than that. In the prediction the step "PE's own busy time is 509.93 against 488.8, so 21.1 of the excess is work of the side chains (and some slow clock)" should have set the work apart from the clock.

*Second: the stops that were to stay.* "I take 20" for the first batch, "half of it, 2.6" of the remaining waits for `hid_lo` and "I take 16" left 23 of 54 us of idle time in the batches of tiles; 9.7 stayed. With 21.3 instead of 20 in the attention, this is 14.6 us. The cuts for "stages that are late for another reason" had no row behind them. Most of this is the table's: e7, with all the parts that were priced by a row, still has 112.2, 85.9 and 72.1 us, against the forecast's 104, 80 and 72; the table was never costed as a part of its own. The 13.85 at `xq` were put down to POOL's products and to the later transposes together; with the products gone and before's ticks, e7 still stands there for 8.2. With half 0's 3.1 the other way, 19.2 + 14.6 - 3.1 is the 31 us between forecast and result.

*The rival that gave the time.* "PE comes near its floor" had 1411, from 36 us of idle time less in the attention and 50 in the feed forward. Measured are 21.3 and 44.3 of idle time, and 24.2 of busy time that it didn't have. Its time is right in part by luck.

*The place in the head.* The mechanism was right and the best supported part: 23.8 expected, 4.2 left. The give-back of 4 us was fair for the idle time (21.3 to 21.7 measured).

*Products on VectorE.* Median 0.541 us as taken, but 9 of 48 took over 1 us and two 3.52; the mean is 0.82, under the 1.2 that was named. "Nothing for the path" was wrong for the two: they and the small operation cost 17 us in three heads, of which e4's half 1 got 10.1 back. So the starving rival was true in kind at three places in a kernel that was still 6% faster; its price held for these and not for all 32. The sentence "small operations should be at 0.2 us with no 4 us among them" was wrong: one took 3.26. What was missed in [rows 5] is how long such a hold lasts: the 4.01 us ended 0.03 us after POOL's `q_tmp` did, the last of four POOL operations in a row. The end of a head 0 is another such place, with three.

*The roundings.* Nothing on the path: right in the changed table (e2 even gives them 4.5 us), and wrong in before's (e16).

*x2T of B1.* 7 us forecast, 6.3 measured. The end of 16.8 us stayed.

## What to carry to other kernels

Price a PE stop above its length: here two fifths more on average, 0.4 or 1.8 us for a single one of 1.91; and split PE's busy time into work and clock before calling the rest work. Before moving a VectorE stage to a new place, read what POOL does there: an operation with two SBUF inputs, or a `tensor_scalar` from SBUF to SBUF, can be held until POOL's row of operations ends (3.5 us behind three of them, 6.60 behind seven), where a reduction or an operation with a PSUM input ran through. When several engines run in a hand-made order, one stage moved at a time can move the stop to the next engine (e14, e16); what was worth 36 us was the whole table, finer cuts and ticks together.

## What the runs showed of the hardware that was not expected

- An operation of VectorE of 0.16 us can be held through three POOL operations, 3.26 us, and one of 0.2 through seven, 6.60 us (e6); POOL's next operation went ahead of it each time, until POOL paused. At 592.82 another product was held for 1.29 us only, and there POOL's next operation was the copy into `r_rep`.
- Seven equal stops of 1.91 us did not cost the same: the granted clock stayed at 1.00 behind one and fell to 0.68 over the 4 us behind the next, in turn.
- The same stops in heads 58 and 59 met a clock of 1.00 in the changed kernel and 0.85 in e4, which has fewer stops before them; and one program (half 1 of e1 and e8), idle for the same time, had 5.2 us more of PE's busy time in one execution than in another.
